# One stage for the edge scatter and the row sums of a graph network's first layer, on one Trainium2 core

## The reference

```python
h = x @ Wn.T + bn
a = leaky_relu(sum((h[src] + e) * attn, -1), 0.01)
m = segment_max(a, dst); a = exp(a - m[dst])
a = a / (segment_sum(a, dst)[dst] + 1e-16)
out = relu(segment_sum(h[src] * a, dst))        # 3125 x 256
x = x + out
y = layernorm(x); logits = y @ L0_ffn_Wr        # router of the experts
```

## Time and profile before

| what | us |
|---|---|
| median of 3 runs (3910.45 to 3913.43) | 3912.19 |
| the profiled execution's own time | 3913.0 |
| span of that execution, first to last instruction | 3910.9 |
| `edge_matrices`, first set on DVE to last clearing on ACT | 384.4 to 844.5 |
| `sum_rows`, first matmul to last copy of logits | 845.0 to 1144.2 |

### The profile page before, as it was taken

The page is one execution under the profiler, slowest core; times in us unless marked ns, Lnnn a source line. Parts: engine busy times, 40 slices in busy tenths (PEclk is TensorE's granted clock), DMA queues, the critical chain, the costliest instruction groups (busy, mean ns, idle before and its releaser), DMA issues. The chain is left out here.

```text
span 3910.9 us, 67937 instructions
## 1 busy us (share of the span) xinstructions
PE 3354.7 (86%) x20953; PEld 2798.0 (72%) x20954; DVE 2660.1 (68%) x4956; ACT 2539.5 (65%) x6511; POOL 817.6 (21%) x454
## 2 busy tenths in 40 slices
PE   5674777779978999995799999999999987999674
PEld 3332444458867899985688888888888876887553
DVE  6997999941232300015999999999999627997523
ACT  3894268961113344434899999999999787996331
POOL 3895000000004211100211111111111111111253
PEclk9555999989989999995899999999999998999687
DMA  4893145553424111124011111111110151331225
GB/s 120 195 220 74 55 184 226 235 239 135 151 89 128 49 62 62 62 81 169 23 50 50 48 49 50 50 50 50 50 50 33 45 219 68 131 120 45 84 87 163
DMA packets 109354, 395.86 MB, mean 101 GB/s; under 512 B 12844, under 2 KB 67926, under 8 KB 85958
## 3 DMA queue, kind: packets, MB, share of 16 engines
q1 hardware_dynamic: 95040, 356.38, 26.5%
q0 software_dynamic: 11824, 31.87, 2.6%
q10 hardware_dynamic: 2368, 6.03, 0.7%
HBM read 269.67 MB, written 124.57 MB: 101 GB/s over the span
## 5 line engine op out<-in xcount | busy, mean ns | idle before, releaser
L1439 PE MATMUL gat_agg<-f_XN,gat_A 128*128 128x257 f32 x5000 | 1109.0, 380 | 20.1 <-DVE gat_A L1560 20.1
L1439 PEld LDWEIGHTS gat_agg<-f_XN,gat_A 128*128 128x128 f32 x5000 | 938.0, 190 | 154.8 <-DVE gat_A L1560 20.8
L1360 ACT ACTIVATE kept_X<-kept_X,gat_s 128x128 f32<-128x128 f32 x2500 | 741.7, 392 | 71.1 <-DVE kept_X L1549 71.0
L1305 POOL TENSOR_TENSOR kept_X<-gat_low,gat_r 128x1024 f32<-128x1024 f32 x100 | 245.5, 2455 | 1140.5 <-DVE gat_A L1560 691.8
L2551 ACT ACTIVATE moe_exp_h<-moe_exp_hbank,w_b1c 128x128 f32<-128x128 f32 x632 | 231.9, 368 | 365.3 <-PE moe_exp_hbank L2495 310.0
L1549 DVE SCALAR_TENSOR_TENSOR kept_X<-gat_r,gat_s 128x128 f32<-128x128 f32 x1700 | 457.0, 348 | 5.0
L920 PE MATMUL mat_cw<-mat_join,mat_lane 128*128 128x400 f16 x1184 | 323.6, 340 | 118.3 <-DVE mat_join L885 55.0
L1560 DVE SCALAR_TENSOR_TENSOR gat_A<-kept_X,early_C 128x1664 f32<-128x1664 f32 x200 | 356.4, 1824 | 0.5 <-ACT kept_X L1360 0.5
L1513 DVE CUSTOM_DVE_ANT_0 kept_X<-gat_als,gat_absT 128x3200 bf16<-128x3200 f32 x96 | 334.3, 3483 | 0.1
L2622 DVE TENSOR_TENSOR moe_exp_xgT<-moe_exp_ybank,moe_b 128x256 f32 x109 | 46.3, 425 | 415.9 <-PE moe_exp_ybank L2504 390.1
L923 PE MATMUL mat_cw<-mat_join,mat_lane 128*128 128x200 f16 x1184 | 299.3, 253 | 0.0
(11 more groups left out here) (393 smaller groups left out, 5361.7 us busy)
## 6 DMA issues: line engine op xcount, KB each, us to landing
weight_matrix<-w_wide SPq DMA_DIRECT2D x25, 1600.0 KB, 5.2
count_matrix<-w_wide SPq DMA_DIRECT2D x25, 1600.0 KB, 8.7
early_C<-count_matrix SPq DMA_DIRECT2D x25, 1600.0 KB, 6.6
late_C<-count_matrix SPq DMA_DIRECT2D x25, 1600.0 KB, 6.6
w_wide<-in_edge_attr_dram SPq DMA_DIRECT2D x50, 768.0 KB, 6.5
e_WT<-weight_matrix SPq DMA_DIRECT2D x13, 1600.0 KB, 6.7
sum_more<-weight_matrix SPq DMA_DIRECT2D x12, 1600.0 KB, 6.7
moe_exp_xgT<-slot_rows SPq DMA_DIRECT2D x20, 640.0 KB, 9.5
```

The costliest lines, as they stand in the source:

```text
L1305: nc.gpsimd.tensor_tensor(work[h % 2][:, (NT - POOL_TILES) * P:NT * P].rearrange("p (t d) -> p t d", d=P), low[:, :].rearrange("p (t d) -> ...
L1360: last = nc.scalar.activation(w, w, ACT.Exp, bias=s02[:, t, h:h + 1])
L1439: last = nc.tensor.matmul(agg[h % 2][:, 0:D + 1], A[h % 2][:, t, :], g.XN[:, t, :], start=(t == 0), stop=(t == NT - 1))
```

## The change

`edge_matrices` and `sum_rows` become one function, `scatter_and_sum`.

- A set has 8 items instead of 16 and there are four sets, in two rounds of two. Which round's half of `lane` and `join` is meant (`slot`) is the turn's number modulo 2, held in a register, on DVE and on PE.
- The scatter's loop is written out once for each tile, 25 times on PE and on DVE, each with its bounds in registers: it takes rounds of 16 items up to the last full round of the tile; the rest falls to the next tile's loop. The bounds are loaded once, 25 registers.
- Behind the loop of tile i PE sums tile i - 1, straight from the SBUF copy that ACT made. The weight matrix is no longer stored and read back; the count matrix still is stored.
- The scatter has six PSUM banks, so three pairs, instead of eight. The bank is worked out beforehand in `prepare` (five small DVE instructions) and stands in the low three bits of the item's word. One bank holds the sum, and one holds the transposed rows and all the logits, which are copied once at the end.
- DVE adds tile i - 2 to `X` behind its sets for tile i; ACT's root, normalisation and copy for tiles i - 2, i - 3 and i - 5 stand behind its eight pairs of tile i. The normalised rows go through a ring of four and are stored tile by tile; `route` no longer stores them.
- The first layer's expert weights take room that is now free (`m.spare`); what loads them, and when, stays.

The core of the diff, without the plain moves:

```diff
-U = 16
+U = 8
-BANKS = 8
+BANKS = 6
+ALL_BANKS = 8
+ROUNDS_HELD = 2
+AHEAD = ROUNDS_HELD * 2 * U
...
+            link(nc.vector.tensor_scalar(sixth_i[:, :], b_n[:, :], 1.0, float(SIXTH), ALU.add, ALU.mult))
+            link(nc.vector.tensor_scalar(sixth_i[:, :], sixth_i[:, :], 16, None, ALU.logical_shift_right))
+            link(nc.vector.tensor_copy(sixth[:, :], sixth_i[:, :]))
...
+        def lane_of(slot, b):
+            return (lane[:, bass.ds(slot, 1), b * 2 * U * P:(b + 1) * 2 * U * P]
+                    .rearrange("p o (w u l) -> p (o w) u l", w=2, u=U))
+        def join_of(slot, b):
+            return (join[:, bass.ds(slot, 1), b * 2 * U * JW:(b + 1) * 2 * U * JW]
+                    .rearrange("p o (u w j) -> p (o u) w j", w=2, u=U))
+        def bounds(eng):
+            ends = [eng.alloc_register(f"rounds{t}") for t in range(NT)]
+            eng.wait_ge(rounds_ready, 1)
+            eng.load(ends, rounds[0:1, 0:NT])
+            return [0] + [eng.snap(r, min_val=1, max_val=SLOTS // (2 * U)) for r in ends]
...
+            for i in range(NT + 3):                                     # DVE
+                if tile_in(i):
+                    with dve.Fori(until[i], until[i + 1]) as it:
+                        for b in range(2):
+                            make_set(it, b)
+                if tile_in(i - 2):
+                    add_sums(i - 2)
+                if tile_in(i - 3):
+                    scales(i - 3)
...
-            with strides(pe, SLOTS // U, 2) as it:
-                mine = block_of(0)
+            def items(it):                                              # PE
+                mine = block_of(0)
+                slot = pe.snap(it % ROUNDS_HELD)
+                for b in range(2):
+                    lanes, joins = lane_of(slot, b), join_of(slot, b)
+                    for n in range(U):
+                        at_item = b * U + n
+                        if at_item % LOAD == 0:
+                            load_blocks((at_item // LOAD + 1) % len(blocks), it * (2 * U) + (at_item + LOAD))
+                        if n == 0:
+                            pe.wait_ge(set_ready, it * 2 + (b + 1))
+                        pe.wait_ge(drained, mine)
+                        bank = pe.snap(mine % ALL_BANKS)
...
-                        nc.tensor.matmul(banks[:, bass.ds(bank, 1), 0:2 * JW]..., lane[:, b, 0, n, :],
-                                         join[:, b, n, :, :]...)
+                        nc.tensor.matmul(banks[:, bass.ds(bank, 1), 0:2 * JW]..., lanes[:, 0, n, :],
+                                         joins[:, n, :, :]...)
+                        nc.tensor.matmul(banks[:, bass.ds(bank, 1), 0:JW]..., lanes[:, 1, n, :],
+                                         joins[:, n, 1, :], ...).then_inc(item_done, 1)
...
+            for i in range(NT + 6):                                     # PE
+                if tile_in(i):
+                    with pe.Fori(until[i], until[i + 1]) as it:
+                        items(it)
+                if tile_in(i - 1):
+                    sum_tile(i - 1, behind)      # 25 matmuls; in their middle project(i - 6), turn(i - 5)
```

More of the change, by code:

```diff
@@ L262, in _ @@
             last.then_inc(turned_ready, 1)
[L263 removed]
+            pe.wait_ge(b_ready, 2)
             for n in range(GROUPS):
[L265 removed]
+                last = nc.tensor.matmul(row[:, n * P:(n + 1) * P], word_n[:, n:n + 1], g.ident[:, :], start=True, stop=True)
             last.then_inc(row_ready, 1)
@@ L852, in edge_matrices @@
[L852 to L855, removed]
-        def pairs(hot):
-            return hot.rearrange("p u (l t) -> p u l t", t=2)
-        def every_pair(values, n):
-            return values.rearrange("p (u o) t -> p u o t", o=1).to_broadcast([P, U, n // 2, 2])
-        def iota_pairs(iota, n):
-            return iota.rearrange("p (o l t) -> p o l t", o=1, t=2).to_broadcast([P, U, n // 2, 2])
@@ L866, in _ @@
[L866 to L893, removed]
-            last.then_inc(banks_ready, 1)
-            pe.sem_inc(item_done, AHEAD)
-            blocks = [[pe.alloc_register(f"block{q}_{n}") for n in range(LOAD)] for q in range(2 * U // LOAD)]
[L898 to L905, removed]
-            with strides(pe, SLOTS // U, 2) as it:
-                mine = block_of(0)
[L908 to L941, removed]
-                                     [:, :, s * 2 * DB:(s + 1) * 2 * DB].rearrange("p r (e j) -> p e r j", e=2),
-                                     pair.rearrange("p e (r j) -> p e r j", j=DB), ACT.Copy).then_inc(copied, 1)
-                act.wait_ge(copied, i * PAIRS + (s + 1))
-                nc.scalar.activation(pair, clear[:, :].rearrange("p (o j) -> p o j", o=1).to_broadcast([P, 2, 2 * JW]),
[L946 to L975, removed]
@@ L978, in sum_rows @@
[L978 to L982, removed]
+        zeros = clear[0:1, 0:256].bitcast(BF16)
+        rounds = k.sb("rounds", [1, NT], I32)
+        both = [g.wide[:, b * 2 * NT * P:(b + 1) * 2 * NT * P].rearrange("p (w n) -> p w n", w=2) for b in range(HELD)]
         rden = k.sb("rden", [P, 2])
-        new = k.sb("new", [P, 2, D])
-        more = k.sb("more", [P, ROWS_IN - ROWS_EARLY, NT * P])
-        rows = [g.WT[:, b, :] for b in range(ROWS_EARLY)] + [more[:, b, :] for b in range(ROWS_IN - ROWS_EARLY)]
+        fresh = k.sb("fresh", [P, D])
@@ new lines, in scatter_and_sum, with pairs, every_pair, iota_pairs @@
+        stored = [k.sem(f"stored{b}") for b in range(HELD)]
+        xn_out = [k.sem(f"xn_out{b}") for b in range(XN_KEPT)]
+        block = ctx.enter_context(nc.Block())
+        def pairs(hot):
+            return hot.rearrange("p u (l t) -> p u l t", t=2)
+        def every_pair(values, n):
+            return values.rearrange("p (u o) t -> p u o t", o=1).to_broadcast([P, U, n // 2, 2])
+        def iota_pairs(iota, n):
+            return iota.rearrange("p (o l t) -> p o l t", o=1, t=2).to_broadcast([P, U, n // 2, 2])
@@ new lines, in _, with load_blocks @@
+            for b in range(BANKS):
+                last = nc.tensor.matmul(cw[:, b * 512:(b + 1) * 512], zeros[:, 0:P], zeros[:, :], start=True, stop=True,
+                                        skip_group_check=True)
+            last.then_inc(banks_ready, 1)
+            pe.sem_inc(item_done, AHEAD)
+            blocks = [[pe.alloc_register(f"block{q}_{n}") for n in range(LOAD)] for q in range(2 * U // LOAD)]
+            def load_blocks(q, first):
+                pe.load(blocks[q], g.item_block[0:1, bass.ds(first, LOAD)])
@@ new lines, in project, with sum_tile @@
+            def project(t):
+                pe.wait_ge(xT_ready, t + 1)
+                for c in range(KD):
+                    last = nc.tensor.matmul(small[:, t * E:(t + 1) * E], m.xT[:, c, t * P:(t + 1) * P], wr[:, c, :],
+                                            start=(c == 0), stop=(c == KD - 1))
+                last.then_inc(prod_ready, 1)
+            def sum_tile(t, behind):
+                pe.wait_ge(copied, (t + 1) * PAIRS)
+                if t >= 1:
+                    pe.wait_ge(fresh_ready, t)
+                else:
+                    pe.wait_ge(b1_kept, 1)
@@ new lines, in _ @@
+            for i in range(NT + 5):
+                if tile_in(i):
+                    act.load(ends, g.pair_end[0:1, i * PAIRS:(i + 1) * PAIRS])
+                    if i >= HELD:
+                        act.wait_ge(stored[i % HELD], i // HELD * 16)
+                        act.wait_ge(sum_done, i - HELD + 1)
+                    for s in range(PAIRS):
+                        drain(i, s)
+                if tile_in(i - 2):
+                    root(i - 2)
+                if tile_in(i - 3):
+                    norm(i - 3)
+                if tile_in(i - 5):
+                    keep_turned(i - 5)
```

272 lines of the change are left out of this document (166 added, 106 removed).

## The result

The changed kernel takes 4127.13 us (median of 4 runs, 4124.65 to 4128.47) against 3912.81; the ratio is 1.0547 (1.0534 to 1.056), 214 us more. I had forecast 3985 us, within 3880 to 4060. The direction is right, the size is not: 214 us instead of 73. The number of the second rival, 4127, is the one that came.

A forecast was written before the change was run, and what follows sets the result against it. PE's sequencer was to bound the merged stage: 389 + 16 x 7.8 + 288 + 58 x 7.8 - 90 + 29 + 15 + 9 = 1217 us against 1144, 73 longer; 3912.2 + 73 = 3985 us, range 3880 to 4060.

The forecast's parts named there:

- the second rival: PE's sequencer in the scatter: separate instruction for each address, 0.45 us or more an item, 4127 us; chance 0.06.
- What bounds the merged stage: Merged scatter and sum: PE's sequencer needs 7.8 us a round, DVE 5.9, so DVE waits from the second round.
- So I expect one more register instruction for each item: PE's sequencer, scatter: a second instruction ahead of the second matmul, a longer first one; 0.33 us an item, today 0.17.
- A separate instruction for each address: The second rival, on PE's sequencer: 0.45 us or more an item, 142 us on top, 4127; chance 0.06.
- The upper bound of 0.57: PE's sequencer, one scatter item: four separate address instructions, 0.17 + 4 x 0.1 = 0.57 us.
- A round: PE's sequencer, 16 scatter items with two register loads, waits and the loop's end: 7.8 us.
- Run-ahead: PE's sequencer begins the next loop 3.9 us early during each of 23 sums: 90 us less.
- Stores: PE's register loads behind the one remaining store: one slow load for each of 24 tiles, 29 us, between 0 and 59.
- The end: After the last sum, the last tile goes through steps that four tiles queue for: 9 us instead of 5.4.
- ACT and three pairs: Two-round loops: waits for a PSUM bank, ACT 13.2 us against the sequencer's 12.9; 15 us added, 0 to 30.
- Free addresses: Rival, PE's scatter: addresses by slot cost nothing, an item stays at 0.17 to 0.2 us, time 3877; chance 0.20.
- Code that has to be fetched: Rival, PE's loop entries: stops of about 2 us for instruction fetches at 24 entries, 49 us, 4034; chance 0.08.

The follow-up runs named there:

- e1: The kernel before with only the change's addressing, a ring of four sets of 8 chosen by the register slot, stages not merged; ratio to before 1.083.
- e3: The changed kernel with its four sets of 8 at constant places, no slot, loop turns of 32 items; ratio to the kernel before 0.9865.
- e6: The changed kernel with PE's sequencer waiting at each loop from the third on until the previous sum has ended; ratio to the kernel before 1.0796.
- e7: As e3, but ACT leaves out clearing each pair of banks, so items add up on old values; ratio to the kernel before 0.9753.
- e5: The changed kernel with only lane chosen by slot and join in two sets at constant places; ratio to the kernel before 1.0384.
- e9: e3 timed again on a chip where the kernel before takes about 3910 us; ratio to the kernel before 0.9872.
- e11: As e3, but POOL does one of DVE's four instructions for a set, the scaling of lanes; ratio to the kernel before 1.001.

## Why the prediction was wrong, by its own steps

- **What bounds the merged stage: right.** That PE's sequencer would take over, DVE be held and sums stay as they were, is what the trace shows. e1 and e3 show it from both sides: the addresses alone cost more than the whole change, and without them the change gains.
- **"So I expect one more register instruction for each item": this failed.** There are two more. From today's 88 ns I made one instruction of 0.144 us that does bank, `lane` and `join` of the first matmul. It is two, 78 and 101 ns, with a way between them. The second matmul's 74 ns is exactly as worked out, and so are about 15 ns for an operation and the gaps. The full working with the product redone gave 0.37 us; I took 0.33, nearer to a product that is kept; with 0.37 the forecast would have been 4032. Measured: 0.47. Over 1184 items 0.14 us is 166 us; the whole miss is 4127 - 3985 = 142 us, since the smaller terms together came out lower.
- **The rival's number was right by luck, its picture half.** "A separate instruction for each address", 0.45 us or more, is not what is there: the four addresses by slot cost two more instructions, not four. That its 4127 is the measured time to the microsecond comes of 0.02 us an item too little and smaller terms too high. What I held against it, that L2495 does one address in one instruction with two operations, still holds; it shows what one address costs and nothing of how much fits in one instruction. The upper bound of 0.57 was sound, and 0.06 for a case inside my own bounds was too little. The range was too narrow even by the sum's own bounds: 0.40 us an item, with stores and ACT at their highest, makes 3985 + 83 + 30 + 15 = 4113, and it ended at 4060.
- **A round**: 7.8 forecast, 9.9 measured. The two loads and waits are 1.8 us (1.96 forecast); the loop's end 0.5 as taken, with 74 more instructions on L1037, one a round, of some 0.1 us.
- **First item** 393.1 instead of 389, since the load of 25 bounds and the set follow each other. **Sums** 290 us for 288. **Run-ahead** 97 by e6 for 90; read from the changed kernel's own trace, 3.95 us at each of 23 sums, it is 91. By an estimate from the 64 places of the Trainium skill, "Advanced Engine Details and Errata", Engine Queue Depths, it could have been 163 us; the run without it shows 97.
- **Stores** 10 slow loads instead of 24, some 12 us instead of 29. **The end** 10.7 us from the last sum to the last logits instead of 9.
- **ACT and three pairs**, 15 us forecast: hardly there. The sum with the measured terms is 393.1 + 158.6 + 290 + 58 x 9.94 - 97 + 12 + 10.7 = 1344; 1360.6 was measured, and it is tempting to put the 17 us left down to ACT. The sequencer's own instructions say otherwise. In the 23 loops after the first sum the gap ahead of the instruction that waits for a bank (L1019) is longer than usual by under 4 us in all, once by 0.5 us and else by under 0.2. With constant addresses such waits do stand there: the same gaps of e3 are together some 80 us above the usual one, up to 2 us each, and without the clearing 37 us, with a stage 42 us shorter (e7). What the 17 us are: the 23 loops take 595.8 us on the sequencer instead of 58 x 9.94 + 12 = 588.5, by many delays of under 0.2 us, and the 23 stretches between loops 177.3 us instead of 23 x 11.6 - 97 = 170, the run-ahead being 91 here. That leaves 2 us.
- **Free addresses**: not there, as e1 and e5 show. Its number, 3877 for a stage that gets rid of them, is 18 us above what the version with constants needs (3859 in e9).
- **Code that has to be fetched**: out. Each of the 25 loop entries is one register move of 29 to 43 ns with the next instruction 0.09 us after its start, and e3, with a body of twice the length, is the quickest of the complete kernels. Between 386 and 1361 us, 23 transfers of instructions went to PE's queue q8 (one in the earlier trace rows), and none held it up measurably.

One thing stays open: why the first matmul's arithmetic is cut in two. Both the number of operations that fit in one register instruction and the way the program is lowered would do it; no run tells them apart.

## What to carry to other kernels

Before a loop's buffers are chosen by a register, count the sequencer's instructions for one turn, their durations and the 0.07 us behind each, and set the sum beside the engine that hides them now; a merge takes such cover away. Unroll until the ring's places are constants: here the same merge with a body of 32 items is 1.3% faster than before and the one with `slot` 5.5% slower. And where a row shows what one address costs, it does not yet show what five cost together: keep the upper bound in the range.

## What the runs showed of the hardware

- An address by register costs about 30 ns on PE's sequencer, an instruction about 0.1 us with the way to the next, and with 0.47 us of such work an item the array at full clock, 0.25 us an item, waits for it (e5, e1).
- With 0.47 us from item to item PE was granted 0.75 (e1, 549 to 1163 us), and in the stretches at 1.2 GHz its item took 0.50 us instead of 0.25; in e3's head, where the array was busy 74 of 100 us, it was granted 0.95. The slow clock cost nothing in e1: turns at 0.66 and at 1.00 both took 10.0 us, because the sequencer set the pace.
- DVE's fp16 product of 1600 values took 2.48 us beside a POOL instruction of 2.46 us, 0.98 alone (e11): work given to the idle engine made the busy one slower.
